# A graph layer on one core: early rows' layers, counts and one-hots in another order, and one unread product a step

## The chip, the cores and the metric

The kernel runs on one core of a Trainium2 chip. The metric is the device time in microseconds of one execution. TensorE multiplies matrices into PSUM, VectorE and ScalarE work elementwise, GpSimd issues the gathers, and SyncE (SP) issues the other transfers; each engine runs its own list of instructions in order, and they wait for one another on semaphores.

## The reference

A message passing layer over 6,250 nodes of 128 features and 100,000 edges, sorted by their target `dst` (low targets are more frequent):

```python
a_k = exp(relu(e @ W_att_k + b_att_k))          # e = [h[src], h[dst]], k = 1, 2, 3
avg_a = (a_1 / att_1[dst] + a_2 / att_2[dst] + a_3 / att_3[dst]) / 3   # att_k = segment sums of a_k
m = avg_a * relu(relu(relu(h[src] @ W1 + b1) @ W2 + b2) @ W3 + b3)
h_neigh = segment_sum(m, dst) / max(deg, 1)
out = relu([h, h_neigh] @ W_c1 + b_c1) @ W_c2 + b_c2
return layernorm(x + out)
```

## The kernel before

*Nodes first.* The three message layers and the attention logits are computed once per node into a table of rows (`message_table`). The edges are cut into groups of 256 (391 groups, two tiles of 128 edges each). The first 94 groups (`n_hot`) go to the most frequent targets and are not gathered: a later stage weights whole blocks of nodes by how often each occurs as a source, from a matrix `counts`.

*Units and steps.* The other 297 groups are taken in 126 units, one per step of a loop that every engine runs: unit 0 has two groups, units 1 to 23 four ("long"), the rest two. GpSimd gathers the rows of a tile with one indirect DMA (L1224) into a ring of eight places; a long unit takes two places, and a gather may only start when the unit that held its place has been added by TensorE. TensorE makes logits and one-hot masks of a unit (`edge_q`, L1357, two steps ahead), VectorE makes the weights (`logits_of`, `weights`, L1803 to L1834), TensorE multiplies (`add_edges`, L1405 and L1409), and VectorE adds the result to `acc` (`add_sums`, L1851).

*Counts.* In steps 0 to 23 (`COUNT_STEPS`) four hot groups a step are counted: VectorE makes one-hots of the source block (`one_hots`, L1695), ScalarE those of the low part of the index (`low_hots`, L1553, L1558), TensorE multiplies them (`count_edges`, L1426, two products a group into one of four banks), and in the next step VectorE adds the banks to `counts` (`add_counts`, L1708). The widths grow with the group: 294, 441 and 490 columns. Each addition waits for the one before it.

*Early rows.* For nine long units ("early", 4, 6, ..., 20) the second half of the rows isn't gathered from the table. Their `x` rows are gathered during the node stage and kept; SP loads one block per two steps (`load_early`, L1273, once the third layer has freed the buffer), TensorE turns it (`turn_early`, L1372), ScalarE copies it (L1586), and the layers follow: `first_early` (L1379, 512 columns), ScalarE's `hidden_early` (L1592), `second_early` (L1384, 512 columns), `hidden_early`, `third_early` (L1390), VectorE's `rows_early` (L1819) and ScalarE's `relu_early` (L1597). The products share one bank.

*The order of TensorE's step.* It is written out by hand. Even step: `add_edges`, `third_early` of the block before, `count_edges`, `turn_early`, `edge_q`. Odd step: `add_edges`, `first_early`, `count_edges`, `second_early`, `edge_q`. SP's round loads near nodes, logit parts, then the early block, then (in rounds 13 to 15) stores single columns of hot logits (L1305).

*After.* From step 27 to 77 the hot blocks are weighted (L1518, L1730, L1443) beside the short units, then the last layers of finished nodes.

Of the kernel before, what the change touches and what calls it, by code (L numbers as in the profile page):

```python
# [32 lines left out]
P = 128  # L33
# [29 lines left out]
EARLY_FROM, EARLY_EVERY = 4, 2  # L63
# [29 lines left out]
def gnn_program(nc, x, x_t, src, dst, w_first, w_rest, b_rows, table, hot_table, near_table, q_table, early_table, out,  # L93
# [59 lines left out]
    with ctx:  # L153
# [908 lines left out]
        def edge_pass(first):  # L1062
# [146 lines left out]
            with Straight(nc) if first else nc.Block() as block:  # L1209
# [22 lines left out]
                def _(sp):  # L1232
# [60 lines left out]
                    for at in range(-AHEAD, n_steps):  # L1293
                        while loaded < n_units and taken(loaded, NEAR) <= at + 1:
                            load_near(loaded)
                            loaded += 1
                        if at + AHEAD + Q_RING - 2 < n_units:
                            load_q(at + AHEAD + Q_RING - 2)
                        if first and at > 0 and at % EARLY_EVERY == 0 and at // EARLY_EVERY < EARLY:
                            load_early(at // EARLY_EVERY)  # L1300
# [29 lines left out]
                def _(pe):  # L1330
# [82 lines left out]

                    def count_edges(step):

                        for g in range(step * PAIRS, min((step + 1) * PAIRS, n_hot)):
                            n = width_of(g) * n_blocks
                            pe.wait_ge(s_lo, g // TWO + 1)
                            if g >= FOUR:
                                pe.wait_ge(s_cadd, g - FOUR + 1)  # L1420
                            if g == LEFT_NEXT:
                                pe.wait_ge(s_left, len(LEFT_STEPS) + 1)
                            for h in range(TILES):
                                t = g * TILES + h
                                pe.wait_ge(s_oh, t + 1)
                                pe.matmul(bank[COUNT_BANKS[g % FOUR]][:, 0:n], hot_lo[:, t % HOT_RING, :],  # L1426
                                          hot_comb[:, t % HOT_RING, 0:n], start=h == 0,
                                          stop=h == TILES - 1).then_inc(s_ct, 1)
# [38 lines left out]
                    for i in range(n_steps):  # L1467
# [3 lines left out]
                        if i + 2 < n_units and not (first and i < COUNT_STEPS):  # L1471
                            edge_q(i + 2)
                        if k is not None and i % EARLY_EVERY == 0 and k >= 1:
                            third_early(k - 1)
                        if k is not None and i % EARLY_EVERY == 1 and k < EARLY:
                            first_early(k)
                        if first and i < COUNT_STEPS:
                            count_edges(i)
                        if k is not None and i % EARLY_EVERY == 0 and k < EARLY:
                            turn_early(k)  # L1480
                        if k is not None and i % EARLY_EVERY == 1 and k < EARLY:
                            second_early(k)
                        if i + 2 < n_units and first and i < COUNT_STEPS:
                            edge_q(i + 2)
# [13 lines left out]
                def _(act):  # L1498
# [110 lines left out]
                    for i in range(n_steps):  # L1609
                        if first and 0 <= i - HOT_AT - 1 < n_blocks:  # L1610
                            hot_exp(i - HOT_AT - 1, 1)
                        if i + 1 < n_units:
                            mask_copy(i + 1)
                            exps(i + 1)
                        if first and i < COUNT_STEPS:
                            low_hots(i)
                        k = early_turn(i)
# [5 lines left out]
                        if k is not None and i % EARLY_EVERY == 1 and k < EARLY:  # L1623
                            hidden_early(k, 0)
                            hidden_early(k, 1)
# [16 lines left out]
                def _(dve):  # L1642
# [44 lines left out]
                    def one_hots(step):  # L1687

                        for g in range(step * PAIRS, min((step + 1) * PAIRS, n_hot)):
                            n = width_of(g) * n_blocks  # L1690
                            if g >= PAIRS:
                                dve.wait_ge(s_ct, (g - PAIRS + 1) * TILES)
                            for h in range(TILES):
                                t = g * TILES + h
                                dve.tensor_scalar(hot_comb[:, t % HOT_RING, 0:n], iota16[:, 0:n],  # L1695
                                                  comb_t[:, g, h:h + 1], None, ALU.is_equal).then_inc(s_oh, 1)

                    def add_counts(step):
                        if step == 0:
                            dve.wait_ge(s_zero, zeroed)  # L1700
                        for g in range(step * PAIRS, min((step + 1) * PAIRS, n_hot)):
                            w = width_of(g)
                            start = hot_window(g)
                            dve.wait_ge(s_ct, (g + 1) * TILES)
                            if g >= 1:
                                dve.wait_ge(s_cadd, g)
                            here = counts[:, :, bass.ds(start, w)]
                            dve.tensor_tensor(here, here, bank[COUNT_BANKS[g % FOUR]][:, 0:w * n_blocks].rearrange(  # L1708
                                "p (b d) -> p b d", d=w), ALU.add).then_inc(s_cadd, 1)
# [149 lines left out]
                    for i in range(n_steps):  # L1859
# [5 lines left out]
                        if first and 0 <= i - 1 < COUNT_STEPS:  # L1865
                            add_counts(i - 1)
                        if first and i < COUNT_STEPS:
                            one_hots(i)
# [140 lines left out]
```

## Time and profile before

| what | us |
|---|---|
| median of three runs | 831.94 (829.34 to 834.98) |
| profiled execution, its own time | 827.13 |
| its span in the trace | 823.1 |
| mean granted clock of TensorE | 0.856 |

Times in the trace count from the start of the span. "Busy" is the union of an engine's instructions; a number in square brackets behind an instruction is how long its engine stood idle before it and what ended that. PEclk is the granted share of TensorE's 2.4 GHz, so 0.50 is 1.2 GHz.

### The profile page before, as it was taken

The numbers are of one execution on the slowest core, as the hardware profiler recorded it, in microseconds if no ns is written. First come the engines' busy times: TensorE is split into PE (matmuls) and PEld (weight loads), VectorE is DVE, ScalarE is ACT, GpSimd is POOL, SyncE is SP. The second block draws the span as 40 slices with busy tenths as digits, with TensorE's granted clock in tenths as the row PEclk, the third lists the DMA queues.
The fourth block names the chain that finished last, engine by engine and source line by source line (L and its number), as shares of the span: only waits on it lengthen the run. The fifth ranks groups of instructions, "written<-read, shape, count | busy, mean of one in ns | idle before, by whom it ended". The sixth has DMA issues, their size and how long they took to land.

```text
span 823.1 us, 17406 instructions
## 1 busy us (share of the span) xinstructions
PE 685.3 (83%) x5133; PEld 534.5 (65%) x5133; DVE 589.1 (72%) x1943; ACT 419.8 (51%) x1048; POOL 571.6 (69%) x605
## 2 busy tenths in 40 slices
PE   9933899999698777899998988888788888779875
PEld 5732566666366444698787777777676667657664
DVE  5883667676677678677777777677667777787766
ACT  6556566666555342677777767664123322332323
POOL 7777776555544677777777777777777777777760
PEclk9975777778777677699999999999889999898898
DMA  7873333222652223333333333333434343343321
GB/s 234 244 186 74 80 80 77 63 63 63 58 43 54 55 66 94 73 87 76 87 77 84 79 80 77 82 80 91 108 91 115 101 106 102 103 132 99 100 57 33
DMA packets 82741, 75.14 MB, mean 91 GB/s; under 512 B 34872, under 2 KB 66400, under 8 KB 82640
## 3 DMA queue, kind: packets, MB, share of 16 engines
q0 software_dynamic: 19008, 39.82, 22.1%
q1 hardware_dynamic: 63344, 34.00, 14.9%
q8 instruction: 44, 0.72, 0.4%
q14 instruction: 57, 0.47, 0.2%
q10 hardware_dynamic: 288, 0.13, 0.1%
HBM read 64.62 MB, written 9.26 MB: 90 GB/s over the span
## 4 chain that ended last, share of the span: by engine, by line
PE 27%; DVE 23%; POOL 18%; issue 16%; ACT 7%; DMA 6%; DVEq 2%; SPq 1%; ACTq 0%
POOL work L1224 18%; PE bank L1405 7%; DVE fin L1730 7%; ACT bank L1518 4%; DMA hot_logit<-early_rows 3%; DVE counts L1708 2%; PE bank L1426 2%; DVE acc L1851 2%; PE bank L881 2%; DVE fin L1695 2%; PE bank L1409 2%; DMA work<-message_table,src_t 2%; PE bank L1361 2%; PE bank L599 2%; PE bank L1379 1%
## 5 line engine op out<-in xcount | busy, mean ns | idle before, releaser
L1224 POOL DMA_INDIRECT work<-message_table,src_t x558 | 530.8, 951 | 214.5 <-issue 164.6
L1405 PE MATMUL bank<-work 128*128 128x144 f32 (+8 forms) x1188 | 235.9, 329 | 38.5 <-DVE acc L1851 38.3
L1405 PEld LDWEIGHTS bank<-work 128*128 128x128 f32 x1188 | 186.1, 222 | 60.0 <-issue 45.8
L1579 ACT COPY work<-bank 128x192 f32<-128x192 f32 (+7 forms) x126 | 37.3, 296 | 189.2 <-DVE work L1803 189.0
L1443 PE MATMUL bank<-work,fin 128*128 128x129 f32 (+1 forms) x882 | 114.7, 286 | 0.0
L1851 DVE TENSOR_TENSOR acc<-acc,bank 128x192 f32 (+8 forms) x297 | 88.7, 299 | 30.4 <-issue 7.5
L1518 ACT ACTIVATE bank<-hot_logit 128x384 f32<-128x384 f32 (+1 forms) x147 | 72.7, 494 | 69.2 <-DVE fin L1730 60.2
L1443 PEld LDWEIGHTS bank<-work,fin 128*128 128x128 f32 (+1 forms) x882 | 105.5, 197 | 2.1
L1834 DVE TENSOR_TENSOR work<-bank,work 128x576 f32<-128x576 f32 (+7 forms) x126 | 86.2, 684 | 13.5 <-DVE work L1829 0.5
L1730 DVE SCALAR_TENSOR_TENSOR fin<-bank,counts 128x384 f32<-128x384 f32 (+1 forms) x147 | 81.4, 554 | 17.3 <-ACT bank L1518 16.4
L1409 PE MATMUL bank<-work 128*4 128x48 f32 (+8 forms) x1188 | 92.9, 203 | 0.0
L1509 ACT ACTIVATE hot_logit<-logits_or_x,work 128x384 f32<-128x384 f32 (+1 forms) x147 | 88.3, 600 | 0.0
L881 PE MATMUL bank<-rest_w,acc 128*128 128x128 f32 x294 | 51.3, 340 | 34.1 <-DVE fin L972 26.9
L1708 DVE TENSOR_TENSOR counts<-counts,bank 128x294 f32 (+2 forms) x94 | 57.4, 611 | 21.8 <-DVE counts L1708 13.6
L1409 PEld LDWEIGHTS bank<-work 128*4 128x4 f32 x1188 | 49.0, 87 | 36.3 <-issue 7.2
L1426 PE MATMUL bank<-fin 128*128 128x294 bf16 (+2 forms) x188 | 53.1, 424 | 19.7 <-ACT fin L1558 13.2
L881 PEld LDWEIGHTS bank<-rest_w,acc 128*128 128x128 f32 x294 | 45.6, 242 | 36.3 <-DVE fin L972 28.0
L1357 PE MATMUL bank<-side 48*128 48x57 bf16 (+8 forms) x594 | 41.7, 186 | 21.2 <-DMA side<-logit_parts 18.7
L1553 ACT ACTIVATE fin<-fin 128x128 bf16<-128x128 f16 x188 | 59.3, 387 | 0.0
L1426 PEld LDWEIGHTS bank<-fin 128*128 128x128 bf16 x188 | 21.1, 118 | 54.7 <-issue 23.5
L1761 DVE TENSOR_SCALAR side<-side,less_col 48x512 bf16<-48x512 bf16 x149 | 53.8, 373 | 3.3 <-DMA side<-near_nodes 3.2
L1829 DVE TENSOR_SCALAR work<-work 128x12 f32<-128x12 f32 (+1 forms) x126 | 24.4, 194 | 42.6 <-ACT work L1539 41.5
(150 smaller groups left out, 811.1 us busy)
## 6 DMA issues: line engine op xcount, KB each, us to landing
work<-message_table,src_t POOLq DMA_INDIRECT x558
side<-near_nodes SPq DMA_DIRECT2D x102, 48.0 KB
side<-logit_parts SPq DMA_DIRECT2D x297, 0.8 KB
message_table<-work SPq DMA_DIRECT2D x12, 262.0 KB, 3.8
work<-message_table SPq DMA_DIRECT2D x48, 65.5 KB
work<-in_x_t SPq DMA_DIRECT2D x12, 256.0 KB, 4.0
fin<-in_x SPq DMA_DIRECT2D x11, 256.0 KB, 3.1
logits_or_x<-in_x_t SPq DMA_DIRECT2D x11, 256.0 KB
```

Of the source, the lines that this page charges most:

```text
L881: last = pe.matmul(to[:, k * P:(k + 1) * P], acc[:, k, nodes], wc1[:, 1, :], start=True, stop=True)
L1224: pool.indirect_dma_start(out=rows_of(n)[:, t, :], out_offset=None, in_=table[:, :], in_offset=bass.IndirectOffsetOnAxis(ap=src_t[:, h, g: ...
L1405: pe.matmul(sums[:, at:at + HEADS * w], rows_here[:, t, 0:P], wt_of(i)[:, t, :], start=h == 0, stop=h == TILES - 1)
L1409: last = pe.matmul(sums[SUMS_AT:SUMS_AT + HEADS + 1, at + HEADS * w:at + HEADS * w + w], a_col[:, i % THREE, t, :], mask_of(i)[:, t, :], s ...
L1426: pe.matmul(bank[COUNT_BANKS[g % FOUR]][:, 0:n], hot_lo[:, t % HOT_RING, :], hot_comb[:, t % HOT_RING, 0:n], start=h == 0, stop=h == TILES ...
L1443: last = pe.matmul(bank[SIDE_BANKS[h]][:, k * (P + 1):(k + 1) * (P + 1)], hot_wt[0:m, b % THREE, k, h * P:(h + 1) * P], rows_here, start=F ...
L1509: act.activation(hot_logit[0:m, n % TWO, :], hot_ld[0:m, k, :], ACT.Relu, bias=hot_block[0:m, b % BLOCKS, 1 + P + k:2 + P + k]).then_inc(s ...
L1518: act.activation(bank[EXP_BANK][0:m, 0:hot_nodes], hot_logit[0:m, n % TWO, :], ACT.Exp).then_inc(s_he, 1)
L1708: dve.tensor_tensor(here, here, bank[COUNT_BANKS[g % FOUR]][:, 0:w * n_blocks].rearrange("p (b d) -> p b d", d=w), ALU.add).then_inc(s_cad ...
L1730: dve.scalar_tensor_tensor(hot_wt[0:m, b % THREE, k, :], bank[EXP_BANK][0:m, 0:hot_nodes], FLT_MAX, counts[0:m, b, :], ALU.min, ALU.mult). ...
L1834: dve.tensor_tensor(wt_of(i).rearrange("p t (k w) -> p t k w", w=w), from_q(i)[:, :, PARTS:PARTS + w].unsqueeze(2).to_broadcast([P, n, HEA ...
L1851: dve.tensor_tensor(here, here, sums[:, at:at + (HEADS + 1) * w].rearrange("p (k w) -> p k w", w=w), ALU.add).then_inc(s_acc, 1)
```

## The change

- The early units become 3, 5, ..., 19.
- TensorE's even step: `add_edges`, `count_edges`, `turn_early`, `edge_q`, `first_early`. Odd step: `add_edges`, `second_early`, `count_edges`, `edge_q`, `third_early` of the same block.
- At the head of `count_edges` a product of 256 columns with 128 weights (`keep_busy`) into the bank that the step's first group then overwrites; nothing reads it. It is left out in step 19, whose bank is in use.
- ScalarE does the first hidden layer before `low_hots`.
- VectorE adds the counts of one group and makes the one-hots of the next in turn (`count_step`).
- SP issues `load_early` at the head of its round.

```diff
-EARLY_FROM, EARLY_EVERY = 4, 2
+EARLY_FROM, EARLY_EVERY = 3, 2
...
                     for at in range(-AHEAD, n_steps):
+                        if first and at > 0 and at % EARLY_EVERY == 0 and at // EARLY_EVERY < EARLY:
+                            load_early(at // EARLY_EVERY)
                         while loaded < n_units and taken(loaded, NEAR) <= at + 1:
...
-                        if first and at > 0 and at % EARLY_EVERY == 0 and at // EARLY_EVERY < EARLY:
-                            load_early(at // EARLY_EVERY)
...
+                    def keep_busy(step):
+
+                        g = step * PAIRS
+                        if g >= FOUR:
+                            pe.wait_ge(s_cadd, g - FOUR + 1)
+                        if g != LEFT_NEXT:
+                            pe.matmul(bank[COUNT_BANKS[g % FOUR]][:, 0:2 * P], w3, rest_w[:, P:3 * P],
+                                      start=True, stop=True)
+
                     def count_edges(step):
 
+                        keep_busy(step)
...
-                        if i + 2 < n_units and not (first and i < COUNT_STEPS):
-                            edge_q(i + 2)
-                        if k is not None and i % EARLY_EVERY == 0 and k >= 1:
-                            third_early(k - 1)
                         if k is not None and i % EARLY_EVERY == 1 and k < EARLY:
-                            first_early(k)
+                            second_early(k)
                         if first and i < COUNT_STEPS:
                             count_edges(i)
                         if k is not None and i % EARLY_EVERY == 0 and k < EARLY:
                             turn_early(k)
+                        if i + 2 < n_units:
+                            edge_q(i + 2)
+                        if k is not None and i % EARLY_EVERY == 0 and k < EARLY:
+                            first_early(k)
                         if k is not None and i % EARLY_EVERY == 1 and k < EARLY:
-                            second_early(k)
-                        if i + 2 < n_units and first and i < COUNT_STEPS:
-                            edge_q(i + 2)
+                            third_early(k)
...
+                        k = early_turn(i)
+                        if k is not None and i % EARLY_EVERY == 1 and k < EARLY:
+                            hidden_early(k, 0)
                         if first and i < COUNT_STEPS:
                             low_hots(i)
...
                         if k is not None and i % EARLY_EVERY == 1 and k < EARLY:
-                            hidden_early(k, 0)
                             hidden_early(k, 1)
...
+                    def count_step(i):
+
+                        for j in range(PAIRS):
+                            if 0 <= (i - 1) * PAIRS + j < n_hot:
+                                add_counts((i - 1) * PAIRS + j)
+                            if i * PAIRS + j < n_hot:
+                                one_hots(i * PAIRS + j)
...
-                        if first and 0 <= i - 1 < COUNT_STEPS:
-                            add_counts(i - 1)
-                        if first and i < COUNT_STEPS:
-                            one_hots(i)
+                        if first and i <= COUNT_STEPS:
+                            count_step(i)
```

## Rows read from the trace of the kernel before

**Rows 1.** The page: an engine's busy time, and its slices of the span.

```profile
PE 685.3 (83%) x5133; PEld 534.5 (65%) x5133; DVE 589.1 (72%) x1943; ACT 419.8 (51%) x1048; POOL 571.6 (69%) x605
...
POOL 7777776555544677777777777777777777777760
PEclk9975777778777677699999999999889999898898
```

**Rows 2.** Waits of GpSimd, 55 to 313 us and 313 to 802: total, times, longest.

```profile
POOL work L1224 <- PE bank L1409: 47.4, 10, 12.9
...
POOL work L1224 <- PE bank L1409: 2.1, 7, 0.3
```

**Rows 3.** Timeline of GpSimd: start, duration, instruction, idle before it and its releaser.

```profile
166.14 0.94 POOL L1224 DMA_INDIRECT work<-message_table,src_t  x1 [5.28 <-PE bank L1409]
167.38 0.95 POOL L1224 DMA_INDIRECT work<-message_table,src_t  x1 [0.30 <-issue]
...
280.52 1.01 POOL L1224 DMA_INDIRECT work<-message_table,src_t  x1 [3.34 <-PE bank L1409]
...
311.92 0.94 POOL L1224 DMA_INDIRECT work<-message_table,src_t  x1 [1.53 <-PE bank L1409]
...
799.11 0.94 POOL L1224 DMA_INDIRECT work<-message_table,src_t  x1 [0.30 <-issue]
```

**Rows 4.** Stretches, cut where TensorE starts units 2, 8, 14, 15, 16, 19; two between clock changes.

```profile
core 0: us, PE busy (x) PEld busy (x) DVE busy (x) ACT busy (x) POOL busy (x), PEclk, DMA share, GB/s
92.50:151.00 58.50, 53.61 (x364) 39.28 (x360) 39.77 (x135) 38.10 (x103) 40.93 (x44) 0.77 0.30 75
151.00:212.50 61.50, 58.07 (x365) 38.64 (x361) 45.32 (x135) 40.24 (x103) 35.05 (x37) 0.78 0.32 63
212.50:228.70 16.20, 9.81 (x71) 7.45 (x69) 7.95 (x23) 6.53 (x17) 6.71 (x8) 0.78 0.58 63
228.70:239.90 11.20, 11.20 (x53) 6.84 (x53) 8.41 (x24) 5.55 (x15) 4.43 (x5) 0.56 0.46 21
239.90:274.80 34.90, 29.05 (x189) 20.02 (x186) 28.33 (x74) 17.80 (x48) 20.61 (x22) 0.82 0.33 63
119.16:129.40 10.24, 10.24 (x51) 7.66 (x51) 5.89 (x21) 6.36 (x17) 7.61 (x9) 0.50 0.29 65
129.40:139.64 10.24, 8.59 (x77) 6.28 (x74) 7.39 (x25) 6.35 (x17) 7.80 (x9) 1.00 0.36 90
```

**Rows 5.** Timeline of TensorE, steps 5 and 6, and of step 14.

```profile
121.10 1.09 PE L1405 MATMUL bank<-work 128*128 128x60 f32 x4
...
126.14 2.08 PE L1379 MATMUL bank<-work,fin 128*128 128x512 f32 x2
...
129.70 1.02 PE L1384 MATMUL bank<-hot_logit,logits_or_x 128*128 128x512 f32 x2
...
130.94 0.66 PE L1405 MATMUL bank<-work 128*128 128x60 f32 x4
...
134.03 1.16 PE L1390 MATMUL bank<-rest_w,hot_logit 128*128 128x128 f32 x8
...
136.67 0.68 PE L1426 MATMUL bank<-fin 128*128 128x294 bf16 x4 [0.98 <-ACT fin L1558]
138.01 0.66 PE L1372 MATMUL bank<-ident,hot_logit 128*128 128x128 f32 x4 [0.67 <-DMA hot_logit<-early_rows]
...
224.96 1.12 PE L1372 MATMUL bank<-ident,hot_logit 128*128 128x128 f32 x4 [5.42 <-DMA hot_logit<-early_rows]
```

**Rows 6.** Timeline of SP's issues around step 14.

```profile
206.57 1.37 SPq L1305 DMA_DIRECT2D hot_logits<-per_node  x3
...
216.81 0.35 SPq L1273 DMA_DIRECT2D hot_logit<-early_rows  x1
217.21 1.38 SPq L1305 DMA_DIRECT2D hot_logits<-per_node  x3
```

**Rows 7.** Timeline of VectorE in step 22.

```profile
308.23 0.67 DVE L1708 TENSOR_TENSOR counts<-counts,bank 128x490 f32 x1 [0.20 <-DVE counts L1708]
309.10 0.67 DVE L1708 TENSOR_TENSOR counts<-counts,bank 128x490 f32 x1 [0.20 <-DVE counts L1708]
309.68 2.36 DVE L1695 TENSOR_SCALAR fin<-fin 128x490 bf16<-128x490 f16 x8
```

More of the change, by code:

```diff
@@ L1614, in _ @@
                             exps(i + 1)
+                        k = early_turn(i)
+                        if k is not None and i % EARLY_EVERY == 1 and k < EARLY:
+                            hidden_early(k, 0)
                         if first and i < COUNT_STEPS:
                             low_hots(i)
-                        k = early_turn(i)
                         if k is not None and i % EARLY_EVERY == 0:
@@ L1685, in _ @@
                     hot_window = window_registers(dve, n_hot, lambda g: hot_nodes - width_of(g))
[L1687 to L1696, printed above, removed]
@@ L1698, in add_counts, with one_hots @@
-                    def add_counts(step):
-                        if step == 0:
-                            dve.wait_ge(s_zero, zeroed)
[L1701 to L1709, printed above, removed]
+                    def one_hots(g):
+                        n = width_of(g) * n_blocks
+                        if g >= PAIRS:
+                            dve.wait_ge(s_ct, (g - PAIRS + 1) * TILES)
+                        for h in range(TILES):
+                            t = g * TILES + h
+                            dve.tensor_scalar(hot_comb[:, t % HOT_RING, 0:n], iota16[:, 0:n],
+                                              comb_t[:, g, h:h + 1], None, ALU.is_equal).then_inc(s_oh, 1)
@@ new lines, in add_counts @@
+                    def add_counts(g):
+                        if g == 0:
+                            dve.wait_ge(s_zero, zeroed)
+                        w = width_of(g)
+                        start = hot_window(g)
+                        dve.wait_ge(s_ct, (g + 1) * TILES)
+                        if g >= 1:
+                            dve.wait_ge(s_cadd, g)
+                        here = counts[:, :, bass.ds(start, w)]
+                        dve.tensor_tensor(here, here, bank[COUNT_BANKS[g % FOUR]][:, 0:w * n_blocks].rearrange(
+                            "p (b d) -> p b d", d=w), ALU.add).then_inc(s_cadd, 1)
```

## Prediction

> **What bounds the kernel now.** I read the page first, then GpSimd's waits, then its timeline, then the stretches of the long steps on every engine, and last the order of single instructions within a step.
>
> The page says that no engine is full over the whole span, and that the granted clock of TensorE goes up and down during the first 40% [rows 1]. GpSimd's row is what to look at: its slices dip from the sixth to the fourteenth and are level from there to the end [rows 1]. The list of waits puts numbers on it: up to 313 us the gathers waited 47.4 us for L1409, the last product of an edge unit, in 10 waits; after it 2.1 us in seven, none longer than 0.3 [rows 2]. That 0.3 is the ordinary distance between two gathers (each 0.94 us, the next starts 1.25 us later [rows 3]). So from 311.9 us, where the last real wait (1.53) ends [rows 3], GpSimd issues gathers without a break until 800 [rows 3], and what follows is a tail of fixed work. The end is set by how much GpSimd waits before 312 us. Of the 47.4 us, 3.0 are the ordinary distance (10 x 0.3), so 44 us is all that faster long steps can ever give.
>
> Each of these waits is for a free place in the ring of gathered rows, freed when TensorE has done add_edges of the unit eight places back. So the price of a long step (steps 0 to 23) is paid one for one, up to the end of add_edges(19), which released the gather at 280.52. From there GpSimd needs 30 us for 24 gathers and meets add_edges(22) with 1.5 us of wait left [rows 3], so steps 20 to 22 can give only about 1.5 us, plus what is shared.
>
> What a long step costs: six steps 2 to 7 take 58.50 us, TensorE busy 53.61; six steps 8 to 13 take 61.50, TensorE 58.07; VectorE has 39.8 and 45.3 [rows 4]. There TensorE binds, and at a mean granted clock of 0.77 and 0.78: nearly half of the time at 1.2 GHz. In steps 16 to 18 (34.9 us) VectorE carries the longer rounds: 28.33 us busy, plus the pauses of its own additions and register loads. Step 14 lasts 16.20 us with TensorE busy 9.81 [rows 4]; it waited 5.42 us for the load of an early block [rows 5].
>
> **Part by part.**
>
> *The clock.* Between 119.16 and 129.40 TensorE is busy all the time at 0.50; from 129.40 to 139.64 it has 1.00 and is busy 8.59 of 10.24 [rows 4]. The rows tell why it alternates. The two wide layer products (L1379, L1384) and the count products all fall together in the odd step, and the clock rises at their end. The even step then has the narrow edge products (four of 60 columns), the short third layer, a wait of 0.98 us for ScalarE's low one-hots and 0.67 for the early block, and the clock falls at its end [rows 5]. The change moves one wide product (first_early) to the end of the even step, the third layer to the end of the odd one, and puts a 256-column product behind add_edges. Each narrow stretch then lies between wide ones. I expect fewer falls, not none, since the early unit's logit products and any wait in front of the counts stay quiet stretches. Taken: a quarter of the time at 1.2 GHz where it is now about 0.45. Ends: none, and as now (a half).
>
> The price of a half clock: four L1405 products take 1.09 us at 1.2 GHz and 0.66 at 2.4; two wide ones 2.08 against 1.02 [rows 5]. Between 1.65 and 2.0, nearer to the first since edge products fill most of a step; I use 1.68, which makes the work of a step at full clock 53.61/6 x (0.54 + 0.46/1.68) = 7.3 us in steps 2 to 7 and 58.07/6 x (0.56 + 0.44/1.68) = 8.0 in steps 8 to 13.
>
> The Trainium skill speaks against the unread product. "TensorE: Matmul & The Clock Gate", section "HAM oscillation — how this bites in real kernels", ties a fall of the clock to long waits between bursts; by that rule no fall was due here, the added product could only cost, and the sum would be that of the first rival below. The trace disagrees: the clock fell with no wait above 0.98 us in the step. The same page's "A second HAM failure mode: psum-queue depth-cycling" describes short pauses that suffice, which the rows support.
>
> *The unread product.* 256 columns are half a wide product: 0.51 us at full clock and 1.04 at half (half of the 1.02 and 2.08 of two 512-column instructions [rows 5]), with its weights 0.55 taken. One a step, on the path while TensorE binds: work 7.85 and 8.5 us a step. It brings no new wait: it waits for the addition that frees the bank, which the first count product of the step waits for anyway.
>
> *Waits in even steps.* Now 53.61 of 58.50 busy: 0.8 us idle a step. The 0.67 us for the early block goes: its load is issued once the third layer has freed the block (216.81, behind the near and logit loads [rows 6]), and now that third layer ends one add_edges and one round of counts earlier, with the load first in SP's round. The 0.98 for ScalarE came from hidden layer two, for which ScalarE stood at the end of the odd step; it now has its product before the counts. Left: turn_early still needs VectorE's rows_early, behind the counts, and first_early needs the copy of that turn. Taken 0.35 us a step; ends 0 and 0.8.
>
> So a step at a quarter half clock: 7.85/(0.75 + 0.25/1.68) = 8.7, with idle 9.1 (now 9.75); 8.5 gives 9.45, with idle 9.8 (now 10.25). Six steps each: 3.9 + 2.7 = 6.6 us.
>
> *Step 14.* The stores of hot logits (issued at 206.57 and again at 217.21, 0.4 us behind the early load of 216.81) are 4-byte pieces, and the load between them landed after 8 us [rows 5, 6]. In the new order that load is issued before the second set by some 3 us (the four logit loads stand between) and has a whole add_edges more to land. 16.2 becomes 9.8: 6.4 us. If the first set alone delays it: 1 to 2 us less. Step 15 ran at 0.56 [rows 4]: 11.2 to 9.8, 1.4 us.
>
> *SP's queue.* load_early's wait now stands ahead of the near and logit loads, in each even round. They start later by the third layer and the issue, 1 to 2.5 us; their readers come at least one whole step of 9 us later, so I cost this at nothing. Without that cover it would be the same 1 to 2.5 us in each second step, up to 20 in all.
>
> *VectorE.* The four additions wait 0.20 us for one another, 0.87 from start to start for 0.67 of work [rows 7]; with one-hots between, three such pauses go: 0.6 us a step. The order of ready one-hots also lets TensorE start counting sooner. Could the mixing cost? At most the overlap between like neighbours, under 0.1 us per switch by the overlapping rows (309.68 starts before 309.10 + 0.67 ends), so between 0 and 0.6, taken in full for steps 16 to 18 and 20 to 22, where VectorE binds; in steps 2 to 15 it is hidden by TensorE. Steps 16 to 18: 1.8, with 1.2 of wait for the early block and for the clock: 3.0. Then 1.0 for add_edges(19), partly at full clock, and 1.2 from steps 20 to 22, capped by the ring.
>
> *Early units 3, 5, ..., 19 in place of 4, 6, ..., 20.* Still nine blocks and 558 gathers; the short unit comes one earlier, which gives GpSimd 5 us of lead at the start, where steps 1 to 3 follow their gathers. Nothing taken; up to 3 us of gain is in the range.
>
> **Sum.** 6.6 + 6.4 + 1.4 + 3.0 + 1.0 + 1.2 = 19.6 us, all passed on, since 44 us of GpSimd's wait can be removed. The profiled execution would go from 827.1 (span 823.1) to 807.5. It lies 4.8 below the median of the runs, 831.9, from which the same 19.6 gives 812.3.
>
> **The rivals.**
> *The clock does not care* (chance 0.15). Half the time stays at 1.2 GHz and the product is pure cost. Steps become 7.85/0.798 + 0.35 = 10.2 (+0.4) and 11.0 (+0.75): +6.9; step 14 still gives 5.2, steps 15 to 18 2, the rest 1.2. Result -1.5 us: 830. For it: the dense run of the odd step that raises the clock today is broken up. Against: two such runs a pair take its place, and the added product lengthens both.
> *The clock stays low* (0.05, slower). If the spread runs no longer raise it and 80% of the time is at 1.2 GHz, a step takes 7.85/0.676 + 0.2 = 11.8 and 8.5/0.676 + 0.2 = 12.8: +12 +15; step 14 gives 3.4, the others cost 7. About 862. It decides from a half-clock share of about 0.52. Against: today every full-width run raises it within a pair of steps.
> *The clock hardly falls* (0.20). 8.1 and 8.8 a step: 9.9 + 8.7, step 14 7.4, step 15 2.4, the rest 5.7: 34 us, 798.
> *The forecast* has 0.60: 804 to 822.
>
> **Range and chances.** 797 to 829 leaves out the slow case and half of the unchanged one. A measurement of this kernel can tell about 1% from no change, that is 823.6 to 840.3. Faster: 0.60 + 0.20 and a little of the first rival, 0.82; same 0.13; slower 0.05.
>
> **What would show it.** After the change: GpSimd's waits for L1409 before 313 us down to some 28 us; the clock in steps 2 to 13 near 0.87 with longer stretches at full; no wait of TensorE for the early block and step 14 under 11 us; the 0.20 us pauses between additions gone; the stretch without waits from some 290 us to the end unchanged in length. Wrong would be: a clock at 0.77 or less, one-hots or additions longer than now, or a new wait of VectorE for near loads behind SP's queue.

## The result and the profile after

The changed kernel takes 803.08 us (median of four runs, 801.68 to 805.79), the kernel before 830.64 in the same comparison (829.33 to 834.98): ratio 0.9663, 95% interval 0.9617 to 0.9710. The forecast was 812.3. The profiled execution took 805.79, the slowest of the four, and the one of before (827.13) was its kernel's fastest, so the two traces show 21.3 us (spans 823.1 and 801.8) of a difference of 27.6. Ratios here and below leave out executions that took over 1.5% longer than the fastest of the same kernel.

The page of the changed kernel, the slices that answer to [rows 1]:

```profile
PE 675.8 (84%) x5179; PEld 529.1 (66%) x5179; DVE 583.5 (73%) x1943; ACT 420.4 (52%) x1048; POOL 571.5 (71%) x605
...
POOL 7677777765556777777777777777777777777760
PEclk9985799979868775999999999999898999899797
```

GpSimd's dip is shorter and shallower, and the sixth to tenth slices of the clock read 9, 9, 9, 7, 9 where they were 7, 7, 7, 7, 8. Its waits up to 293 us, which answer to [rows 2]:

```profile
POOL work L1224 <- PE bank L1409: 24.2, 7, 5.1
```

47.4 us have become 24.2. That is the change: the last gather starts at 778.0 us instead of 799.1, and the tail behind it is as long as before (24 us). The last of these waits now ends at 260.09 us; before it ended at 311.92:

```profile
260.09 0.94 POOL L1224 DMA_INDIRECT work<-message_table,src_t  x1 [2.05 <-PE bank L1409]
```

The stretches, cut at the same units 2, 8, 14, 16 and 19 as in [rows 4] (there 14 to 16 is two rows, 16.20 + 11.20):

```profile
94.70:142.30 47.60, 46.16 (x374) 34.55 (x373) 37.92 (x136) 38.97 (x103) 36.02 (x39) 0.96 0.33 85
142.30:198.30 56.00, 53.12 (x374) 37.56 (x373) 44.68 (x138) 40.20 (x106) 37.55 (x40) 0.90 0.39 71
198.30:218.30 20.00, 19.62 (x126) 13.83 (x125) 15.74 (x47) 10.37 (x27) 11.57 (x13) 0.78 0.73 71
218.30:254.70 36.40, 28.28 (x178) 18.61 (x177) 26.55 (x73) 17.15 (x46) 20.74 (x23) 0.81 0.37 60
```

Read the first number and PEclk: steps 2 to 7 gain 10.9 us and run at 0.96 instead of 0.77; steps 8 to 13 gain 5.5 at 0.90 instead of 0.78; steps 14 and 15 gain 7.4; steps 16 to 18 lose 1.5. The start loses 2.2 (unit 2 begins at 94.7, not 92.5). Of the 16.4 us that steps 2 to 13 gain, 4.0 are less idle time of TensorE (8.3 us before, 4.3 now), and 12.4 are less busy time, although the unread product has been added.

One pair of steps on TensorE, which answers to [rows 5]:

```profile
121.44 1.13 PE L1384 MATMUL bank<-hot_logit,logits_or_x 128*128 128x512 f32 x2
122.40 0.59 PE L1420 MATMUL bank<-rest_w 128*128 128x256 f32 x2
122.84 1.27 PE L1436 MATMUL bank<-fin 128*128 128x294 bf16 x8
124.38 0.27 PE L1357 MATMUL bank<-side 48*128 48x29 bf16 x5 [0.28 <-DVE side L1777]
...
126.12 1.14 PE L1390 MATMUL bank<-rest_w,hot_logit 128*128 128x128 f32 x8
127.10 0.55 PE L1405 MATMUL bank<-work 128*128 128x60 f32 x4
...
130.09 0.70 PE L1420 MATMUL bank<-rest_w 128*128 128x256 f32 x2
130.62 1.16 PE L1436 MATMUL bank<-fin 128*128 128x294 bf16 x8
131.62 0.60 PE L1372 MATMUL bank<-ident,hot_logit 128*128 128x128 f32 x4
...
132.90 1.13 PE L1379 MATMUL bank<-work,fin 128*128 128x512 f32 x2 [0.38 <-ACT work L1594]
```

The turn follows the counts without a wait, and what is left is 0.38 us for ScalarE's copy. Nothing else of TensorE waits in the even step. The wait for the early block is gone from every step but one. First two lines of TensorE's waits before (92.5 to 274.8 us: total, times, longest), then those of the changed kernel (94.7 to 254.7 us):

```profile
PE bank L1372 <- DMA hot_logit<-early_rows: 9.6, 6, 5.4
PE bank L1426 <- ACT fin L1558: 6.3, 7, 1.0
...
PE bank L1372 <- DMA hot_logit<-early_rows: 3.8, 1, 3.8
PE bank L1497 <- DVE counts L1716: 3.1, 1, 3.1
PE bank L1379 <- ACT work L1594: 3.0, 8, 0.4
```

The one that is left is in step 16. SP's timeline shows the small stores that lie ahead of the load; that they are the cause is what the late stores below test:

```profile
212.43 2.91 SPq L1305 DMA_DIRECT2D hot_logits<-per_node  x3
218.54 0.32 SPq L1273 DMA_DIRECT2D hot_logit<-early_rows  x1
...
227.57 0.97 PE L1372 MATMUL bank<-ident,hot_logit 128*128 128x128 f32 x4 [3.81 <-DMA hot_logit<-early_rows]
```

VectorE's timeline in step 22, which answers to [rows 7]; the pauses of 0.20 between additions are gone:

```profile
284.64 0.67 DVE L1716 TENSOR_TENSOR counts<-counts,bank 128x490 f32 x1
285.23 0.60 DVE L1703 TENSOR_SCALAR fin<-fin 128x490 bf16<-128x490 f16 x2
285.74 0.65 DVE L1716 TENSOR_TENSOR counts<-counts,bank 128x490 f32 x1
...
289.01 0.17 DVE L1845 TENSOR_SCALAR work<-work 128x24 f32<-128x24 f32 x1
```

From the first addition to the weights that follow the last one-hot it is 4.37 us. In step 22 of the kernel before it was 5.46, 1.1 us more:

```profile
306.50 0.67 DVE L1708 TENSOR_TENSOR counts<-counts,bank 128x490 f32 x1
...
311.96 0.17 DVE L1829 TENSOR_SCALAR work<-work 128x24 f32<-128x24 f32 x1
```

### The profile page after: what moved, and what is told of

The parts are those of the page before. It is cut to its first block, busy times and chain, and to the rows that moved or that the text cites. A ratio compares the mean times of both kernels' runs of the same rounds, so it can differ in the third digit from the quotient of the medians.

```text
span 801.8 us, 17497 instructions
## 1 busy us (share of the span) xinstructions
PE 675.8 (84%) x5179; PEld 529.1 (66%) x5179; DVE 583.5 (73%) x1943; ACT 420.4 (52%) x1048; POOL 571.5 (71%) x605
## 4 chain that ended last, share of the span: by engine, by line
POOL 26%; PE 23%; DVE 18%; issue 17%; ACT 8%; DMA 4%; DVEq 2%; SPq 1%; ACTq 0%
POOL work L1224 26%; DVE fin L1746 7%; PE bank L1405 6%; ACT bank L1526 4%; PE bank L1436 3%; DVE counts L1716 3%; DVE fin L1703 2%; PE bank L1409 2%; DVE acc L1867 2%; PE bank L1361 1%; PE bank L599 1%; DVE work L1845 1%; PE bank L1384 1%; DMA hot_logit<-early_rows 1%; ACT work L1587 1%
## 5 line engine op out<-in xcount | busy, mean ns | idle before, releaser
L1405 PE MATMUL bank<-work 128*128 128x144 f32 (+8 forms) x1188 | 225.6, 318 | 39.8 <-DVE acc L1867 39.6
L1405 PEld LDWEIGHTS bank<-work 128*128 128x128 f32 x1188 | 178.3, 213 | 67.5 <-issue 55.2
L881 PE MATMUL bank<-rest_w,acc 128*128 128x128 f32 x294 | 48.4, 326 | 32.4 <-DVE fin L972 28.5
L881 PEld LDWEIGHTS bank<-rest_w,acc 128*128 128x128 f32 x294 | 43.0, 229 | 34.6 <-DVE fin L972 29.8
L1703 DVE TENSOR_SCALAR fin<-fin 128x294 bf16<-128x294 f16 (+2 forms) x188 | 56.5, 344 | 0.0
L1436 PE MATMUL bank<-fin 128*128 128x294 bf16 (+2 forms) x188 | 47.5, 400 | 7.3 <-ACT fin L1566 4.8
```

Of the source, the lines that this page charges most:

```text
L881: last = pe.matmul(to[:, k * P:(k + 1) * P], acc[:, k, nodes], wc1[:, 1, :], start=True, stop=True)
L1405: pe.matmul(sums[:, at:at + HEADS * w], rows_here[:, t, 0:P], wt_of(i)[:, t, :], start=h == 0, stop=h == TILES - 1)
```

## The experiments

Ratios are to the kernel before, run on the same chip; brackets hold the 95% interval. The changed kernel has 0.9663. Stretches come from one profile each.

**Without the unread product.**

```diff
                     def count_edges(step):
-                        keep_busy(step)
```

> The changed kernel without its unread product. Theory (the product holds the clock up where only narrow edge products would stand): the granted clock of steps 2 to 13 falls from 0.90 back towards 0.8, steps get 0.5 to 1 us longer in spite of the product's 0.55 us that goes, and the time is 805 to 815, ratio to the kernel before 0.97 to 0.98. Rival (the order alone does it, the product is cost): 0.55 us x 14 steps less, 795 to 799, ratio 0.957 to 0.962.

802.50 us, 0.9667 (0.9621 to 0.9714): the same as with the product. The theory's clock and its half microsecond a step came, its time did not; the rival missed. The profile shows why a zero can hide two terms:

```profile
95.60:146.50 50.90, 49.13 (x363) 36.16 (x362) 38.10 (x136) 38.56 (x103) 37.78 (x40) 0.83 0.31 82
146.50:205.30 58.80, 55.82 (x363) 37.25 (x362) 43.43 (x136) 40.00 (x104) 35.70 (x38) 0.80 0.35 65
205.30:222.80 17.50, 16.02 (x122) 10.83 (x121) 16.13 (x49) 11.54 (x30) 10.09 (x11) 0.97 0.60 74
222.80:253.70 30.90, 26.36 (x172) 18.28 (x170) 26.23 (x72) 16.47 (x44) 22.16 (x23) 0.78 0.39 73
```

Without the product the clock of steps 2 to 13 is 0.83 and 0.80, and they take 109.7 us against 103.6. All runs agree on the clock: over the whole program it was 0.875 to 0.880 in the four without the product and 0.881 to 0.890 in the four with it. Then steps 14 to 18 take 48.4 us against 56.4, and no step waits for the early block. That isn't because its load came sooner. In step 16 TensorE stood at half clock (0.58) and asked for the block only 8.1 us after SP issued the load; in the changed kernel it asked after 5.2 us and had it after 9.0:

```profile
223.08 0.32 SPq L1273 DMA_DIRECT2D hot_logit<-early_rows  x1
...
231.17 1.06 PE L1372 MATMUL bank<-ident,hot_logit 128*128 128x128 f32 x4
```

So in these two executions steps 2 to 13 are 6.1 us shorter with the product, its own cost of about 0.5 us a step included, and steps 14 to 18 are 8.0 us longer. Where the 8.0 come from is split up under the late stores.

**The product alone, in the old order.**

In the kernel before, with `keep_busy` as it stands in the change:

```diff
                     def count_edges(step):
 
+                        keep_busy(step)
                         for g in range(step * PAIRS, min((step + 1) * PAIRS, n_hot)):
```

> The kernel before with the unread product at the head of the counts and nothing else. Theory (the product works only where order has already removed the waits of the even steps; here the 0.98 us wait for ScalarE and the early block follow it): the clock keeps its alternation, cost and gain nearly cancel, ratio 0.99 to 1.01. Rival (the product is what lifts the clock, in any order): ratio 0.975 to 0.985.

828.71 us, 1.0008 (0.9974 to 1.0042), as the theory had it. In its profile steps 2 to 7 take 61.8 us at 0.75 and steps 8 to 13 62.6 at 0.78: 4.4 us of cost, and no gain in the clock there. Over the whole program its ten runs lie a little above the thirteen of the kernel before (0.854 to 0.868 against 0.845 to 0.859), which may be why the time shows no cost.

**Counts and one-hots apart again.**

```diff
                         for j in range(PAIRS):
                             if 0 <= (i - 1) * PAIRS + j < n_hot:
                                 add_counts((i - 1) * PAIRS + j)
+                        for j in range(PAIRS):
                             if i * PAIRS + j < n_hot:
                                 one_hots(i * PAIRS + j)
```

> The changed kernel with all additions of counts first and then all one-hots, as before. Theory: VectorE pays three pauses of 0.20 us a step again, which bind in steps 16 to 22 alone, and TensorE gets its first one-hots 2 to 3 us later in the step, which opens a wait in front of the counts in steps 2 to 15 and lets the clock fall more often: 808 to 816, ratio 0.973 to 0.983. Rival (VectorE's order matters only where VectorE binds): 3 us, 806, ratio 0.970.

815.28 us, 0.9849 (0.9809 to 0.9889): 12 to 15 of the 28 us are lost, at the theory's upper end or above it. Its profile, of the fastest of its runs, is only 4.9 us longer than that of the changed kernel, but steps 2 to 13 are 10.6 us longer:

```profile
93.60:147.90 54.30, 51.42 (x375) 38.31 (x375) 39.98 (x136) 38.88 (x104) 38.60 (x41) 0.87 0.30 78
147.90:207.80 59.90, 55.47 (x374) 37.91 (x373) 44.79 (x136) 39.60 (x103) 35.63 (x38) 0.89 0.35 64
```

TensorE's waits are only in small part in front of the counts, where I had put them; more is in front of the logits (93.6 to 259.3 us):

```profile
PE bank L1357 <- DVE work L1851: 2.9, 7, 0.9
PE bank L1357 <- DVE side L1778: 2.4, 3, 0.9
PE bank L1405 <- DVE acc L1868: 2.0, 5, 0.6
PE bank L1436 <- DVE fin L1703: 1.7, 3, 0.8
```

VectorE's weights come behind the whole block of additions and one-hots, and `edge_q` of the next unit waits for them. But TensorE's idle time in steps 2 to 13 grows by only 3.0 us (7.3 against 4.3); the other 7.6 us are busy time, at a clock of 0.87 and 0.89 instead of 0.96 and 0.90. That the waits bring the lower clock with them is likely and not shown.

**A narrow product in place of the wide one.**

```diff
-                            pe.matmul(bank[COUNT_BANKS[g % FOUR]][:, 0:2 * P], w3, rest_w[:, P:3 * P],
-                                      start=True, stop=True)
+                            for _ in range(2):
+                                pe.matmul(bank[COUNT_BANKS[g % FOUR]][:, 0:3], w3, rest_w[:, P:P + 3],
+                                          start=True, stop=True)
```

> The changed kernel with two unread products of 3 columns each in place of one of 256: about the same time on TensorE (0.4 to 0.5 us), hardly any columns. Theory (columns, not mere occupation, hold the clock): as without the product or worse, 808 to 818, ratio 0.973 to 0.985. Rival (anything that keeps TensorE occupied will do): as the changed kernel, 803, ratio 0.966.

814.85 us, 0.9814 (0.9754 to 0.9873), slower than no product at all by 1.5%:

```profile
96.50:161.10 64.60, 63.55 (x387) 48.64 (x386) 37.28 (x133) 37.72 (x100) 36.08 (x39) 0.62 0.24 62
161.10:220.50 59.40, 56.56 (x386) 39.96 (x385) 43.79 (x136) 39.94 (x104) 35.18 (x38) 0.83 0.35 65
```

TensorE is busy 98% of steps 2 to 7, and the clock there is 0.62 against 0.96 in the changed kernel. In all four runs the clock of the whole program is below that of the changed kernel (0.852 to 0.875 against 0.881 to 0.890). The trace shows what lies behind the 0.62: the clock fell at 53 us, in a wait of 15 us before the first unit, as it does at 51 to 54 us in the kernels before and after, where it rises again at 91 us. Here it stayed at half until 141.7, though TensorE stood still for only 0.7 us between 92.0 and 141.4:

```profile
64.42 0.26 PE L1357 MATMUL bank<-side 48*128 48x25 bf16 x4 [15.03 <-DMA side<-logit_parts]
...
92.00:141.40 49.40, 48.70 (x253) 37.71 (x253) 25.28 (x90) 25.36 (x67) 28.25 (x31) 0.50 0.23 60
```

So in these two kernels being occupied didn't bring the clock back. Part of the high busy share is itself the half clock's doing, since the same work then takes longer. The narrow products aren't dearer than the wide one in themselves: at full clock it is 0.36 to 0.47 us from their start to the first count, 0.43 to 0.54 with the wide one. The profile is that of the slowest of the four runs (820.84).

**The small stores four rounds later.**

```diff
-                    HOT_STORES = HOT_AT // 2
+                    HOT_STORES = 17
```

> The changed kernel with the stores of hot logits in rounds 17 to 19 instead of 13 to 15. Theory (these small pieces delay the early block of step 16, a wait of 3.8 us): the wait goes, all of it passed on to GpSimd, 799 to 800, ratio 0.961 to 0.963. Rival (the block is late by other traffic, or VectorE sets step 16 anyway): within 1 us of 803, ratio 0.966.

799.68 us, 0.9645 (0.9598 to 0.9691). The time is the theory's, but the interval of the ratio can't tell it from the changed kernel. What the trace shows is that the wait is gone:

```profile
96.00:144.50 48.50, 47.07 (x375) 36.12 (x375) 37.72 (x136) 38.53 (x104) 36.62 (x40) 0.93 0.34 83
144.50:200.60 56.10, 53.22 (x374) 37.66 (x373) 44.59 (x138) 40.33 (x106) 36.72 (x39) 0.90 0.31 73
200.60:217.50 16.90, 16.52 (x126) 12.16 (x125) 15.24 (x46) 10.43 (x27) 9.90 (x12) 0.94 0.29 70
217.50:249.00 31.50, 27.22 (x178) 17.92 (x176) 26.57 (x73) 16.75 (x45) 22.56 (x23) 0.84 0.69 65
```

No wait for the early block is left, steps 14 to 18 take the same 48.4 us as without the product, steps 2 to 13 keep 104.6, and the span is 793.9. But the 8.0 us aren't all the stores'. The kernel with early registers, further down, keeps the stores' place and waits 3.8 us in step 16 like the changed kernel; its stretches of steps 14 and 15 and of 16 to 18:

```profile
200.80:217.70 16.90, 16.52 (x125) 12.17 (x125) 15.08 (x46) 10.52 (x27) 10.04 (x12) 0.94 0.73 71
217.70:253.60 35.90, 28.09 (x178) 18.67 (x176) 26.94 (x73) 16.97 (x45) 21.97 (x23) 0.81 0.38 67
```

Steps 16 to 18 take 35.9 us in it and 36.4 in the changed kernel, against 31.5 with late stores. These 4.4 to 4.9 us go with the wait and with the half clock behind it in step 17. The other 3.1 us (20.0 against 16.9 in steps 14 and 15) lie ahead of the wait: the clock had fallen in step 13, at 197 us, and came back at 207 in the changed kernel; in the kernel with early registers it fell at 199 and was back at 203. Why one such spell is three times as long as the other isn't shown.

**A product of 512 columns.**

```diff
-                            pe.matmul(bank[COUNT_BANKS[g % FOUR]][:, 0:2 * P], w3, rest_w[:, P:3 * P],
+                            pe.matmul(bank[COUNT_BANKS[g % FOUR]][:, 0:4 * P], w3, rest_w[:, 0:4 * P],
```

> The changed kernel with an unread product of 512 columns. Theory: 0.5 us more a step on TensorE's path in steps 2 to 15, 7 us, and at most 2 to 3 us back from a clock that is then almost always full: 806 to 810, ratio 0.970 to 0.975. Rival (the clock still pays for it): 800 or less, ratio under 0.963.

807.21 us, 0.9746 (0.9701 to 0.9791), as the theory had it. Steps 2 to 13 take 106.6 us at 0.93 and 0.91, against 103.6 at 0.96 and 0.90: the wider product costs 3 us there and the clock isn't higher for it.

**Window registers a step earlier.**

```diff
                         if i == n_units - 1:
                             add_sums(i)
+                        if first and i < COUNT_STEPS:
+                            hot_window.fetch(i * PAIRS)
```

(`fetch` loads the next 16 registers where none are left.)

> The changed kernel with VectorE loading the window registers of the counts at the end of the step before, not at its first addition. Theory (the 1.15 us of that load in steps 5, 9, 13, 17 push VectorE's weights back, TensorE waits 0.76 us in front of the logits and the clock falls right there, at 156 and 193 us): these two falls go, 798 to 801, ratio 0.960 to 0.963. Rival (the stall only changes its place): 803, ratio 0.966.

803.01 us, 0.9697 (0.9655 to 0.9739): the rival. TensorE's waits in front of the logits fall to 0.8 us in total and 2.5 in front of the counts come instead; the clock still falls in steps 9 and 13 (at 162 and 199 us by its records, at 159 and 197 in the changed kernel, not at the 156 and 193 of my expectation). The stall only moved.

**The early load behind the others in SP's round.**

```diff
                     for at in range(-AHEAD, n_steps):
-                        if first and at > 0 and at % EARLY_EVERY == 0 and at // EARLY_EVERY < EARLY:
-                            load_early(at // EARLY_EVERY)
...
                             load_q(at + AHEAD + Q_RING - 2)
+                        if first and at > 0 and at % EARLY_EVERY == 0 and at // EARLY_EVERY < EARLY:
+                            load_early(at // EARLY_EVERY)
```

> The changed kernel with the early block's load behind the near and logit loads of SP's round again. Theory: the load starts some 3 us later and still has the edge products and counts of the even step (6 us) before it is read, so nothing changes but for steps 14 and 16, where the small stores stand: 803 to 807, ratio 0.966 to 0.971. Rival (its place at the head is what removed the waits for it): 812 or more, ratio over 0.977.

810.73 us, 0.9761 (0.9719 to 0.9802): 8 us, between the two. TensorE waits for the early block 5.8 us in five steps, 0.45 to 1.00 of it in each of steps 2, 4 and 6, though no wait was expected outside steps 14 and 16:

```profile
PE bank L1372 <- DMA hot_logit<-early_rows: 5.8, 5, 2.8
PE bank L1379 <- ACT work L1594: 3.0, 8, 0.4
```

The edge products and counts of an even step take 4.5 us at full clock (127.10 to 131.62 in the trace above), not the 6 I counted with. Steps 2 to 13 take 108.1 us instead of 103.6.

**Four more, under other conditions.** During these the kernel before took 1010.78 us (median of 23 runs, 1004.16 to 1128.71), so their ratios are to that and can't be set beside those above. They ran on another chip than the eight above; whether that is the reason wasn't tried. In the profile of each of the four GpSimd stood 127 to 135 us in 85 to 89 pauses that the profile puts to something outside the core. In the second it was this (its waits: total, times, longest; the lines of that kernel lie four further down):

```profile
POOL work L1228 <- remote: 134.9, 89, 4.3
POOL work L1228 <- PE bank L1413: 59.5, 22, 7.3
```

*Late stores without the product.*

```diff
-                    HOT_STORES = HOT_AT // 2
+                    HOT_STORES = 17
...
-                        keep_busy(step)
```

> The late stores, without the unread product. Theory (the product shortens steps 2 to 13 by about 6 us, 109.7 against 103.6 in the two traces, and the wait for the early block in step 16 took that back; with the stores out of the way nothing takes it back): 4 to 7 us slower than the late stores with the product, ratio 0.970 to 0.973. Rival (the product is worth nothing, the 6 us are found in any case by steps 14 to 18): ratio 0.964 to 0.966.

991.30 us, 0.9811 (0.9756 to 0.9867): off both.

*Late stores and early registers.*

```diff
-                    HOT_STORES = HOT_AT // 2
+                    HOT_STORES = 17
...
+                        if first and i < COUNT_STEPS:
+                            hot_window.fetch(i * PAIRS)
```

> The late stores and the window registers of the counts loaded a step earlier. Theory: the two act at different places (step 16; steps 5, 9, 13, 17), but the second was worth under 1 us alone, so 0.5 to 2 us below the late stores alone, ratio 0.962 to 0.964. Rival (the second only moves a stall): ratio 0.9645.

987.08 us, 0.9788 (0.9732 to 0.9845). With the product and the early registers 0.2% less than without them, inside both intervals. Neither this run nor the one before it decides between its expectations. The two traces repeat the product's effect on the clock: steps 2 to 13 take 131.2 us at 0.59 and 0.75 without it, 128.5 at 0.76 and 0.87 with it.

*Counts and one-hots in turn, alone in the kernel before.* (`add_counts` and `one_hots` take a group instead of a step, as in the change.)

```diff
-                        if first and 0 <= i - 1 < COUNT_STEPS:
-                            add_counts(i - 1)
-                        if first and i < COUNT_STEPS:
-                            one_hots(i)
+                        if first and i <= COUNT_STEPS:
+                            count_step(i)
```

> The kernel before with VectorE's counts and one-hots in turn, and nothing else. Theory (the turn pays where TensorE would otherwise wait for its first one-hots, which in the old order of TensorE is hidden by the third or first layer, and in steps 16 to 22 where VectorE binds): 2 to 4 us, ratio 0.995 to 0.998. Rival (the 12 to 15 us that undoing it costs in the changed kernel belong to it in any order): ratio 0.982 to 0.986.

Ratio 0.9937 (0.9880 to 0.9994). Only three of its twelve runs count in this ratio. The median of all twelve, 1015.10 us, lies above the 1010.78 of the kernel before, so no gain of the turn alone is shown here; a gain of 1.4% or more, as in the rival, isn't seen either.

*The order alone.*

The changed kernel without three of its parts: the product, the turn and the early load's place (the first, third and eighth edit above together).

```diff
-                        keep_busy(step)
...
+                        for j in range(PAIRS):
                             if i * PAIRS + j < n_hot:
                                 one_hots(i * PAIRS + j)
```

> The new order of TensorE's and ScalarE's steps and the early units 3 to 19 alone: no product, counts and one-hots apart, the early load behind the others. Theory (order, turn and early load need one another, since each removes a wait that the next would take over): a third to a half of the change, 814 to 820, ratio 0.982 to 0.989. Rival (the order of the layers is the change): 803 to 808, ratio 0.970 to 0.975.

Ratio 0.9843 (0.9796 to 0.9890), from six of its twelve runs; the median of all twelve is 1002.60 us, 0.8% below the kernel before. The ratio lies in the range of its theory and outside the rival's. But runs that vary this much, and an engine held up from outside, which gives each part other covers, make it a hint that the new order alone is worth part of the gain, not a share of the 3.4%.

## Why the prediction was right, and where its working was not

The time moved the way that was forecast and lies in the stated range, but by the medians it fell 27.6 us where 19.6 were forecast. The sum against the profiled execution looks closer than it is: 807.5 forecast, 805.8 measured. It starts from the fastest execution before and ends at the slowest one after, and terms that were wrong in opposite directions nearly cancelled. That closeness is luck; the mechanism, fewer waits of GpSimd, is not.

- *What binds.* Right. The end moved with GpSimd's waits: 23.2 us less wait, a last gather 21.1 us earlier, and 24.2 us of wait left where 28 were forecast. Since the last wait ends at 260.09 us, steps 20 to 23 hold GpSimd up no longer at all.
- *The clock of steps 2 to 13*, 6.6 us in the sum: the term most mis-sized. They gained 10.9 + 5.5 = 16.4 us. The half-clock share was put at a quarter; it was 8% in steps 2 to 7 (0.96) and 20% in steps 8 to 13 (0.90). Put into the prediction's own formula with the idle time that was measured (0.24 and 0.48 us a step), these shares give 11.5 us. The other 4.9 lie in the work of a step at full clock, taken as 7.85 and 8.5 us: steps 5 and 6 of the changed kernel ran at full clock throughout, and TensorE was busy 14.85 of their 15.50 us, 7.4 a step. The order that the mechanism asks for (wide products on both sides of each narrow stretch, no wait but one of 0.38 in the even step) is what the pair above shows. How much of the clock is owed to the order alone was tried only under the other conditions.
- *The unread product.* My text made it part of why the clock stays up, and this holds (0.83 and 0.80 without it, 0.96 and 0.90 with it, 0.62 and 0.83 with narrow ones), but in time it is worth nothing that could be measured in this kernel: 0.9667 against 0.9663. The first rival said that the product would be pure cost with the clock unmoved. In the old order its profile shows this for steps 2 to 13, though the time stayed the same (1.0008); in the new order it is false. The rule of long waits from the Trainium skill ("TensorE: Matmul & The Clock Gate", section "HAM oscillation — how this bites in real kernels") doesn't cover this kernel: the clock fell at 104.9, 159.6 and 197.1 us, and from 94.7 to 198 us TensorE waited nine times and never longer than 0.8 us. The low clock of the narrow products is another case: it began in a wait of 15 us, as the rule has it, and the 49 us of nearly unbroken work behind it didn't end it.
- *Steps 14 and 15*, 7.8 us: measured 7.4.
- *Steps 16 to 18*, 3.0: the one term with the wrong sign. They lost 1.5 us. I moved the early load of step 14 away from the stores and did not ask where the load of step 16 would meet them; it waited 3.8 us there and step 17 then ran at a mean clock of 0.62. With the stores four rounds later these three steps take 31.5 us, 3.4 less than before the change.
- *VectorE's turn*, in the sum with 1.8 us in steps 16 to 18 and at most the 1.2 of steps 20 to 22: far too small. Undoing it costs 12 us by the medians and 15 by the ratios (0.9849 against 0.9663). The 0.6 us a step was short in itself, since 1.1 us went in step 22. And I had costed it on the steps as they were, in which TensorE hid it. With TensorE's step at 7.9 and 9.3 us instead of 9.75 and 10.25 the cover is gone: undoing the turn lengthens steps 2 to 13 by 10.6 us, 0.9 a step.
- *SP's order*, costed at nothing, with 1 to 2.5 us per second step if the cover goes. The load's new place is worth 8 us: the same mistake, since the cover (the even step) had become shorter.
- *add_edges(19) and steps 20 to 22*, 2.2 us: 1.0 came. Unit 19 starts 20.1 us earlier than before and the last gather 21.1.
- *The start*, nothing: 2.2 us lost. No run tried the cause, but the trace shows what was added ahead of unit 2 (steps 0 and 1): the third layer of the first early block (1.1 us at 93.75) and two unread products (2.3 us, at half clock). Without the product the two steps take 25.1 us instead of 25.9, and 23.7 in the kernel before.

The terms of steps 14 to 18, of the start and of the end were together 8.3 us too good (0.4, 4.5, 2.2 and 1.2), and the clock's 9.8 too poor; they nearly cancelled in the profile.

What stays open: the product's own share once the small stores are out of the way. By the profiles steps 2 to 13 are 5 to 6 us shorter with it (103.6 and 104.6 against 109.7 us); the times of the only comparison with late stores, under the other conditions, can't tell it from nothing. Open too is how the gain divides between the new order of the layers and the rest, since the order was never undone alone beside the other parts. The best version by its median is the changed kernel with late stores (799.68), not shown to be faster than the changed kernel.

## What to carry to other kernels

When one engine gets much faster, every step that was costed at little or nothing has to be costed again against the new length of the round: here the order of VectorE's work and a load's place in SP's queue, costed at 3 us or less and at nothing on steps of 10 us, were worth 12 to 15 and 8 us on steps of 8 to 9. If an idle slot is filled to keep TensorE's clock up, try what fills it: here a product of 256 columns went with a higher clock, one of 512 added only cost, and two of 3 columns went with a lower one. A change without an effect on the time should still be looked at by stretches, since 6 us less in some steps and 8 us more in the next can stand behind a zero. And look at a second profile before a stretch's loss is put down to one cause: of those 8 us, 3 were a spell of half clock that another kernel with the same stores didn't have.

## What the runs showed of the hardware

A high busy share didn't go with a high clock. In steps 2 to 7 TensorE's granted clock was 0.62 at 98% busy with two products of 3 columns a step, and 0.96 at 97% busy with one of 256 columns in their place. In the first of these kernels the clock stayed at half from 53 to 141.7 us, the last 49 of them with TensorE idle for 0.7 us in all. It also fell without a long wait: at 104.9 us in the changed kernel, where the only wait since 94.7 was one of 0.4 us.

A load can be late for stores of 4-byte pieces ahead of it. The early block's load, 256 KB, was there 9.0 us after its issue behind such stores (step 16 of the changed kernel), and within 5.1 us of it with the stores moved away (222.75 after 217.70 us).

The same program, the kernel before, took 22% longer in one series of runs (1010.78 us on one chip, 829.24 and 828.65 on two others; whether the chip is the reason wasn't tried). In a trace of that series, of another of the kernels here, GpSimd's gathers pause 1.3 to 1.4 us after every fourth one from 419 to 696 us, and the profile puts these pauses to something outside the core.
